# One batch-by-batch scan stage: first batch reordered, second batch's front beside it, last projection accumulated ahead, step sizes without VectorE's clamp

## The reference

```python
xn = _layernorm(x)
x = x + _L1_attn_ref(xn, ...) + _L1_ffn_ref(xn, ...)

# _L1_attn_ref (a Mamba block), in short
x, z = split(hidden @ in_proj_w.T)
u = silu(causal_conv(x, 4 taps) + conv_b)
dt_low, B, C = split(u @ x_proj_w.T)
delta = softplus(dt_low @ dt_proj_w.T + dt_proj_b)
h = exp(delta * A) * h + delta * B * u        # over 512 steps, 512 channels x 16 states
y = sum over states(h * C) + u * D
out = (y * silu(z)) @ out_proj_w.T

# _L1_ffn_ref: rows and weights are quantised in blocks of 32 to a 6-bit grid, then
out = xd @ wd.T + bias
```

## Time and profile before

| | |
|---|---|
| median of 3 runs | 2140.81 us (2137.47 to 2140.95) |
| profiled execution | 2136.74 us, its span 2134.9 us |
| busy, share of the span | PE 78%, DVE 71%, ACT 47%, POOL 44% |
| VectorE in 40 slices of 53.4 us, tenths | 6446464646465564545217988999999999999995 |
| granted TensorE clock in the same slices | 9999989898989899898686879788797969788576 |
| mix stage | from 1025.9 us on |
| first scan (L1462) | 1133.38 us |
| last gating (L1476) | 2112.34 us |

### The profile page before, as it was taken

The page is one execution under the profiler, slowest core; times in us unless marked ns, Lnnn a source line. Parts: engine busy times, 40 slices in busy tenths (PEclk is TensorE's granted clock), DMA queues, the critical chain, the costliest instruction groups (busy, mean ns, idle before and its releaser), DMA issues.

```text
span 2134.9 us, 22187 instructions
## 1 busy us (share of the span) xinstructions
PE 1675.0 (78%) x6696; PEld 747.9 (35%) x6696; DVE 1522.0 (71%) x2256; ACT 1009.9 (47%) x1542; POOL 943.0 (44%) x676
## 2 busy tenths in 40 slices
PE   7399999999999999999364768687686959687355
PEld 7252626253443535262121224132232414133022
DVE  6446464646465564545217988999999999999995
ACT  3026253443435252525234564757576575757441
POOL 2700000000000000000238778988898898988761
PEclk9999989898989899898686879788797969788576
DMA  5563636344261536260314132433324232432410
GB/s 182 203 103 103 103 100 98 114 76 137 55 134 58 89 105 102 97 113 10 107 59 149 51 111 89 142 123 120 120 99 157 93 125 89 139 128 98 150 50 10
DMA packets 103060, 223.84 MB, mean 105 GB/s; under 512 B 12641, under 2 KB 64994, under 8 KB 99282
## 3 DMA queue, kind: packets, MB, share of 16 engines
q1 hardware_dynamic: 99922, 214.69, 36.2%
q0 software_dynamic: 3072, 8.37, 1.1%
HBM read 169.56 MB, written 53.48 MB: 104 GB/s over the span
## 4 chain that ended last, share of the span: by engine, by line
DVE 22%; PE 14%; issue 7%; POOL 4%; POOLq 2%; DMA 1%; DVEq 1%; ACT 1%; SPq 0%; ACTq 0%
DVE ps L1462 16%; PE ps L1555 6%; DVE work L1468 5%; POOL work L1198 3%; PE ps L1580 2%; PE ps L1587 2%; PE ps L1589 1%; PE ps L1563 1%; PE ps L1591 1%; PE ps L1590 1%; PE ps L1572 0%; POOLq L1246 0%; DVEq L1435 0%; POOLq L1168 0%; DVE xn_step L1442 0%
## 5 line engine op out<-in xcount | busy, mean ns | idle before, releaser
L1198 POOL TENSOR_TENSOR work<-rep,bc 128x1024 f32<-128x1024 f32 x256 | 600.3, 2366 | 116.8 <-PE ps L1580 85.6
L1462 DVE TENSOR_TENSOR_SCAN ps<-ps,work 128x512 f32<-128x512 f32 x512 | 623.5, 1218 | 37.5 <-POOL work L1198 27.5
L1338 ACT ACTIVATE ps<-rep,a_neg 128x512 f32<-128x512 f32 x512 | 345.3, 687 | 315.0 <-DVE work L1468 313.8
L713 DVE TENSOR_REDUCE m<-ps 128x1 f32<-128x512 f32 x512 | 328.2, 686 | 160.3 <-PE ps L819 157.6
L636 ACT ACTIVATE prob<-ps 128x1024 f32<-128x1024 f32 x256 | 257.4, 1022 | 225.7 <-PE ps L843 223.8
L1468 DVE TENSOR_TENSOR work<-ps,bc 128x512 f32<-128x512 f32 x512 | 343.9, 672 | 0.0
L1580 PE MATMUL ps<-work,pick 128*32 128x512 f32 x1024 | 186.1, 810 | 185.3 <-DVE work L1468 185.3
L577 POOL TENSOR_TENSOR m_parts<-m,nil 128x16 bf16<-128x16 f32 x32 | 7.1, 222 | 604.8 <-DVE m L713 604.8
L1555 PE MATMUL ps<-xn_t,in_taps 128*128 128x510 f32 (+3 forms) x512 | 241.3, 627 | 2.2 <-ACT xn_t L1268 1.5
L819 PE MATMUL ps<-k_st,q_st 96*128 96x512 bf16 x512 | 201.0, 437 | 31.2 <-DVE m L713 24.1
L843 PE MATMUL ps<-q_st,k_st 99*128 99x512 bf16 x512 | 166.9, 424 | 0.7
(11 more groups left out here) (176 smaller groups left out, 2058.6 us busy)
## 6 DMA issues: line engine op xcount, KB each, us to landing
rep<-rep_rows SPq DMA_DIRECT2D x128, 512.0 KB, 5.8
w<-in_w SPq DMA_DIRECT2D x32, 1024.0 KB
bc<-bc_rows SPq DMA_DIRECT2D x32, 512.0 KB, 4.7
rep_rows<-inputs SPq DMA_DIRECT2D x32, 512.0 KB, 5.4
qk_parts<-parts SPq DMA_DIRECT2D x96, 128.0 KB
q_st<-qk_parts SPq DMA_DIRECT2D x96, 128.0 KB, 10.5
k_st<-qk_parts SPq DMA_DIRECT2D x96, 128.0 KB, 11.4
dispatch<-zeros SPq DMA_DIRECT2D x4, 1280.0 KB, 10.5
```

The lines of the kernel that those rows point to most:

```text
L713: nc.vector.tensor_reduce(m[:, g % 2, qt, 2 * pair + i:2 * pair + i + 1], ps[:, S0 + i, :], AX.X, ALU.max).then_inc(s_reduced, 1)
L1198: nc.gpsimd.tensor_tensor(work[:, n % WS, :, :], rep[:, g % RS, 2 * h:2 * h + 2, 1, :], bc[:, k, 0, :].unsqueeze(1).broadcast_to([P, 2, SE ...
L1338: nc.scalar.activation(state(m), rep[:, g % RS, 2 * h + i, 0, :], ACT.Exp, scale=a_neg[:, c, 2 * h + i, k:k + 1]).then_inc(decay_ready, 1)
L1462: nc.vector.tensor_tensor_scan(state(m), state(m), work[:, n % WS, i, :], 0.0, ALU.mult, ALU.add).then_inc(state_ready, 1)
```

## The change

- **First batch, other order.** VectorE takes the statistics before the tap weights, and quantises the weights after binade. ScalarE weighs batch 1's expert rows and makes the step sizes before u; the gate projections (z), their Silu and the copy of the turned weights stand behind softplus. TensorE turns the quantised rows before x_proj and projects z after the step sizes; the weights are turned into bank W_FIRST = 3. GpSimd gathers batch 1's rows right after root(0).
- **Second batch's front beside it.** Addition, root, statistics, normalise and transposes of batch 1 are ahead of the loop. LATE is gone: its chain runs at the same offsets as all others. A tiny Exp stands ahead of the loop on ScalarE.
- **Rep load in halves.** `decay` and `drive` wait for two of the four DMAs at each of a chunk's first two pieces.
- **Last output projection ahead.** `out_proj` is split into `out_bias` (one product for the two tiles of a bank, in all batches), `out_known` (quantised rows and x) and `out_gated`. In batch 7 bias, known parts and two gated chunks stand in pieces 20 to 23, the third chunk in pieces 28 to 31, and only the fourth behind the last gating. Every batch is stored in two halves.
- **No clamp on VectorE.** `binade` is one instruction. ScalarE computes max(p − 1, 0) of the power p (`over_one`, one piece before `scale_step`), and the two scalings add the 1 back in their bias. The weights' clamp stays.

```diff
-LATE = 5
...
+W_FIRST = 3
...
-FIRST_PE = {"w": 0, "turn_quant": (1, 2)}
-FIRST_ACT = {"w": 1, "quant": (2, 3), "weigh": 0}
-FIRST_DVE = {"statistics": 2}
-FIRST_POOL = {"add": 2, "root": 4}
+LAST_OUT, LAST_GATED = (20, 21, 22, 23), (28, 29, 30, 31)
...
+        rep_loaded = [[sem(f"rep_loaded_{c}_{h}") for h in range(2)] for c in range(RS)]
...
+            return [(f, n - (f - 1) * PIECES) for f in range(1, BATCH)]
...
+                                     rows.unsqueeze(1).broadcast_to([CH, QUADS, 2 * SEQ])).then_inc(rep_loaded[g % RS][j // 2], 16)
...
-                        sp.wait_ge(out_copied, b * HALVES)
-                        sp.dma_start(io["out"][b - 1].rearrange("(t p) c -> p t c", p=P), x2[:, (b - 1) % XS, :, :]).then_inc(out_stored, 16)
+                        rows = io["out"][b - 1].rearrange("(t p) c -> p t c", p=P)
+                        for h in range(HALVES):
+                            sp.wait_ge(out_copied, (b - 1) * HALVES + h + 1)
+                            sp.dma_start(rows[:, 2 * h:2 * h + 2, :], x2[:, (b - 1) % XS, 2 * h:2 * h + 2, :]).then_inc(out_stored, 16)
...
-                    if q % PER_CHUNK == 0:
-                        pool.wait_ge(rep_loaded[g % RS], (g // RS + 1) * BLOCKS * 16)
+                    if q % PER_CHUNK < 2:
+                        pool.wait_ge(rep_loaded[g % RS][h], (g // RS + 1) * BLOCKS // 2 * 16)
...
+                for i, value in enumerate((-1.0, -2.0 ** -22, 1.5 * 2.0 ** 20)):
+                    nc.gpsimd.memset(shifts[:, i:i + 1], value)
+                nc.gpsimd.memset(idle[:, :], 0.0)
...
                 root(0)
+                pool.drain()
+                place_gather(1)
+                gather(1, range(TT))
                 scale_down(0)
                 for k in range(GRID_STEPS):
                     to_grid(0, k)
                 scale_up(0)
-                pool.drain()
-                place_gather(1)
-                gather(1, range(TT))
+                add_experts(1)
+                root(1)
...
-                    if n == FIRST_POOL["add"]:
-                        add_experts(1)
-                    if n == FIRST_POOL["root"]:
-                        root(1)
...
-                        if f > 1:
...
+                        if at == POOL_AT["gather"]:
...
+                def over_one(f):
+                    act.wait_ge(step_ready, f + 1)
+                    if f == 0:
+                        act.wait_ge(set_up, 1)
+                    nc.scalar.activation(xn_step[:, :, :], xn_step[:, :, :], ACT.Relu, bias=shifts[:, 0:1])
...
+                    act.drain()
...
-                    nc.scalar.activation(nudge, xn_step[:, :, :], ACT.Copy, scale=-2.0 ** -22)
-                    nc.scalar.activation(xn_step[:, :, :], xn_step[:, :, :], ACT.Copy, scale=1.5 * 2.0 ** 20).then_inc(step_scaled, 1)
+                    nc.scalar.activation(nudge, xn_step[:, :, :], ACT.Identity, scale=-2.0 ** -22, bias=shifts[:, 1:2])
+                    nc.scalar.activation(xn_step[:, :, :], xn_step[:, :, :], ACT.Identity, scale=1.5 * 2.0 ** 20, bias=shifts[:, 2:3]).then_inc(step_scaled, 1)
...
                     copy_turned(0, k, k)
+                weigh_experts(1)
+                over_one(0)
+                scale_step(0)
                 for c in range(DC):
                     act.wait_ge(in_done, c + 1)
                     e = nc.scalar.activation(u[:, c, :], ps[:, 2 + c, :], ACT.Silu, bias=conv_b[:, c, :])
                 e.then_inc(u_ready, 1)
-                for c in range(DC):
-                    act.wait_ge(z_done, c + 1)
-                    nc.scalar.activation(sz[:, 0, c, :], ps[:, Z_FIRST[c], :], ACT.Silu).then_inc(z_taken, 1)
+                for k in range(KD):
+                    copy_quant(0, k, k)
                 copy_rows(0, 2)
-                scale_step(0)
                 for c in range(DC):
                     take_dt(0, c, DT_FIRST[c])
                 exponents(0)
                 softplus(0)
+                for c in range(DC):
+                    act.wait_ge(z_done, c + 1)
+                    nc.scalar.activation(sz[:, 0, c, :], ps[:, Z_FIRST[c], :], ACT.Silu).then_inc(z_taken, 1)
+                act.wait_ge(w_turned, 1)
+                nc.scalar.activation(fw_t[:, :, :], ps[:, W_FIRST, :].rearrange("p (k d) -> p k d", d=DM), ACT.Copy).then_inc(w_copied, 1)
+                normalise(1)
                 act.wait_ge(a_ready, 1)
+                nc.scalar.activation(idle[:, :], idle[:, :], ACT.Exp)
+                act.drain()
                 for n in range(BATCH * PIECES):
                     b, q = n // PIECES, n % PIECES
                     decay(b, q)
-                    if n == FIRST_ACT["w"]:
-                        act.wait_ge(w_turned, 1)
-                        nc.scalar.activation(fw_t[:, :, :], ps[:, TB[0], :].rearrange("p (k d) -> p k d", d=DM), ACT.Copy).then_inc(w_copied, 1)
...
-                        weigh_experts(1)
...
+                        if at == ACT_AT["step"] - 1:
+                            over_one(f)
...
                 def binade(f):
                     dve.wait_ge(scaled, f + 1)
-                    nc.vector.tensor_scalar(xn_step[:, :, :].bitcast(I32), xn[:, :, :].bitcast(I32), 0x7F800000, None, ALU.bitwise_and)
-                    dve.drain()
-                    cross = xn_step[:, :, :].rearrange("p t c -> p (t c)").rearrange("p (c i) -> p i c", i=2)
-                    nc.vector.tensor_scalar(cross, cross, 1.0, 4.0, ALU.max, ALU.min).then_inc(step_ready, 1)
+                    nc.vector.tensor_scalar(xn_step[:, :, :].bitcast(I32), xn[:, :, :].bitcast(I32), 0x7F800000, None,
+                                            ALU.bitwise_and).then_inc(step_ready, 1)
...
-                tap_weights()
-                dve.wait_ge(a_exp, 1)
-
-                nc.vector.tensor_scalar(a_neg[:, :, :, :], a_neg[:, :, :, :], -1.0, -1e-30, ALU.mult, ALU.min).then_inc(a_ready, 1)
                 statistics(0)
                 aggregate(0)
+                tap_weights()
                 block_max(0)
                 block_scale(0)
                 binade(0)
+                dve.wait_ge(a_exp, 1)
+
+                nc.vector.tensor_scalar(a_neg[:, :, :, :], a_neg[:, :, :, :], -1.0, -1e-30, ALU.mult, ALU.min).then_inc(a_ready, 1)
                 quantise_weights()
+                statistics(1)
+                aggregate(1)
...
-                    if n == FIRST_DVE["statistics"]:
-                        statistics(1)
-                    if n == FIRST_DVE["statistics"] + 1:
-                        aggregate(1)
...
+                def out_bias(bank):
+                    nc.tensor.matmul(ps[:, bank, :].rearrange("p (t d) -> p t d", d=DM), one_row, bias.unsqueeze(1).broadcast_to([1, 2, DM]),
+                                     start=True, stop=False)
...
+                def out_known(b, t, bank):
                     o = ps[:, bank, (t % 2) * DM:(t % 2) * DM + DM]
...
                     for k in range(KD):
                         nc.tensor.matmul(o, quant_t[:, b % 2, k, t * P:(t + 1) * P], fw_t[:, k, :], start=False, stop=False)
...
+                    nc.tensor.matmul(o, sb["ident"][:, :], x2[:, b % XS, t, :], start=False, stop=False)
...
+                def out_gated(b, t, bank, cs):
+                    o = ps[:, bank, (t % 2) * DM:(t % 2) * DM + DM]
+                    for c in cs:
+                        x = nc.tensor.matmul(o, sz[:, b % 2, c, t * P:(t + 1) * P], out_w[:, c, :], start=False, stop=(c == DC - 1 and t % 2 == 1))
+                    if cs[-1] == DC - 1 and t % 2:
                         x.then_inc(out_done, 1)
+
+                def out_proj(b, t, bank):
+                    if t % 2 == 0:
+                        out_bias(bank)
+                    out_known(b, t, bank)
+                    out_gated(b, t, bank, range(DC))
...
                     pe.wait_ge(w_quant, 1)
+                    pe.wait_ge(dt_taken, DC - 1)
...
+                            x = nc.tensor.transpose(ps[:, W_FIRST, k * DM + t * P:k * DM + (t + 1) * P], fw_raw[:, t, k * P:(k + 1) * P],
...
                 for c in range(DC):
                     in_proj_taps(2 + c, c, range(TAPS), in_done)
-                for c in range(DC):
-                    in_proj(Z_FIRST[c], c, z_done)
+                pe.wait_ge(quant_ready, 1)
+                for k in range(KD):
+                    turn(k, k, quant_turned)
                 project_bc(0, 2)
                 pe.wait_ge(rows_copied, 1)
                 for c in range(DC):
                     project_dt(0, c, DT_FIRST[c])
+                pe.wait_ge(quant_copied, KD)
+                for c in range(DC):
+                    in_proj(Z_FIRST[c], c, z_done)
+                turn_weights()
                 pe.wait_ge(diag_ready, 1)
                 pe.wait_ge(z_taken, DC)
                 pe.wait_ge(dt_taken, DC)
                 pe.wait_ge(set_up, 1)
+                pe.wait_ge(xn_ready, 2)
+                for k in range(KD):
```

(17 more changed lines are left out.)

58 lines of the change are left out of this document (18 added, 40 removed).

## The result

The changed kernel takes 2073.48 us (median of four runs, 2069.07 to 2077.0), against 2139.92 for the kernel before, run beside it. The ratio is 0.969, 95% interval 0.9668 to 0.9712. The forecast was 2080, in a range of 2066 to 2092, so the gain of 66.4 us is 6.6 more than the sum of 59.8.

A forecast was written before the change was run, and what follows sets the result against it. TensorE was taken to bound pieces 0 to 16 of steady batches, with waits at front, seam and tail. Front 17.6, batch 0 9.8, batch 1 15.9, bias 2, tail 14.5 sum to 59.8 us: 2080, range 2066 to 2092.

The forecast's parts named there:

- (a): Front: batch 0's statistics ahead of the tap weights; 1.5 us gained (0 to 4.4), after 2.9 lost to engines blocking.
- (b): Front: gate projections (z) go behind on TensorE, eight passes for quantised rows replace them; 5.6 us gained (5.0 to 6.0).
- (c): Front: scale_step(0) no longer between x_rows and the step-size projections on ScalarE; 0.6 us gained (0 to 0.7).
- (d): Front: GpSimd's first input no longer queued behind quantisation and batch 1's gathers after the Ln; 7.0 us gained (6.5 to 7.1).
- (e): Front: GpSimd's first product starts on half of the rep load; 2.9 us gained (2.0 to 3.0).
- (f): Front: Exp table loaded ahead of the wait; 0 gained, as the first scan waited for the product, not a decay.
- the front is held: Rival: TensorE waits for the quantised rows ahead of x_proj, 6 us lost, 2086 us; chance 0.07.
- Batch 0: Batch 1's statistics 1.8, decay wait 2.5, small scaling 1.7, GpSimd waits 1.2, clamp 2.6: 9.8 us gained (6 to 12).
- the seam stays: Rival: GpSimd's scale_down or inputs for batch 1 come late again, about 11 us, 2091; chance 0.17, wholly or half.
- The clamp in batches 1 to 6: Removing VectorE's clamp there gains 0 of 12.1 us, since it stands inside TensorE's unbroken stretch.
- chief rival: The clamp counts in batches 1 to 6 too, because VectorE bounds them: 12 us less, 2068; chance 0.17.
- The clock: Rival: TensorE's clock left lower for 8.6 us' worth of work in seven batches eats all 60 us; slower 0.03.

The follow-up runs named there:

- taps_first: The changed kernel with the tap weights ahead of the statistics again: mix stage 1046.2 us against 1042.7, first scan 3.1 us later.
- taps_late: The changed kernel with the tap weights held until the root is done: median 2070.18 us, ratio 0.9691; mix stage 1042.5 us against 1042.7.
- rep_full: The changed kernel with decay and drive waiting for all four rep DMAs at a chunk's first piece: mix stage 1045.9 us against 1042.7.
- clamp_back: The changed kernel with VectorE's clamp put back and ScalarE's Relu dropped: median 2076.71 us; mix stage 1047.6 us against 1042.7.
- tail_back: The changed kernel with batch 7's whole output projection behind the last gating, bias still one product: mix stage 1060.6 us against 1042.7, tail 21.7 against 7.4.
- late_back: The changed kernel with batch 1's chain five pieces late again: mix stage 1054.4 us against 1042.7, batch 1's distance 130.23 against 118.73.
- bias_old: The changed kernel with the old output projection in batches 0 to 6 (gated rows first, one bias product a tile): mix stage 1049.8 us against 1042.7.
- relieved pair: The changed kernel with bias, quantised rows and x left out of batches 0 to 6's output projections, without and with VectorE's clamp: mix stage 1033.6 and 1046.6 us.
- queue: The changed kernel with x_proj ahead of the output projection's third and fourth tile: 2063.39 us, ratio 0.9657; mix stage 1033.7 us, with VectorE's clamp 1046.5.

## Why the prediction was right, and where a size was off

- **The front.** (a) 1.5 forecast, 2.2 measured (24.3 to 22.1 us up to the first normalise); the mechanism is shown by taps_first and taps_late. Three of the four operations were expected to pay, 2.9 in all; two did, by 0.9 each, and the power by 0.13, and taps_late puts the loss at 2.1. (b) 5.6 and 5.6, (c) 0.6 and 0.6, (d) 7.0 and 7.0, (e) 2.9 and 2.8, all by the timeline's landmarks, (e) confirmed by rep_full. (f) gains nothing, though only because the load comes later than the decay needs it. The rival that the front is held is out: x_proj waits for u alone.
- **Batch 0.** 9.8 and 9.9, but that they agree so closely is luck. Four terms held: the clamp (2.6 forecast, 2.8 by clamp_back), the statistics, and the waits of 2.48 and 1.04 us, which are gone. One didn't: the small scaling was to give back 1.7 us and takes 2.10 where it took 1.86, again beside a product of GpSimd's. In its place the binade, which was to stay as it was, gave back 1.5: it took 2.54 and takes 1.03. The binade in the timeline of the kernel before:

```profile
1172.63 2.54 DVE L1442 TENSOR_SCALAR xn_step<-xn 128x1024 int32<-128x1024 int32 x1
```

Both in that of the changed kernel:

```profile
1127.02 2.10 DVE L1446 TENSOR_SCALAR absmax<-absmax 128x32 f32<-128x32 f32 x1
...
1139.71 1.03 DVE L1452 TENSOR_SCALAR xn_step<-xn 128x1024 int32<-128x1024 int32 x1
```

- **Batch 1.** 15.9 and 17.5, but 16.4 against tail_back's execution of the same code, whose distance is 119.81: up to 1.1 us of it is where the clock rose. LATE alone is 11.5 (late_back). The new projection has a share, 2.4 by bias_old; the remaining 3.6 were not taken apart. The rival that the seam stays is out.
- **The clamp in batches 1 to 6** at 0, the choice on which the forecast rested against its chief rival: held. By clamp_back the distances differ by -0.1 to 0.4, less than those of two executions of the same code do, and bias_old shows 0 in the steady ones. The rival, 12 us more, would have come near with another queue of TensorE's (10.7 us behind batch 0 in the relieved pair, 10.1 in that of queue).
- **The bias: the term that was mis-sized.** I had "0.35 a batch, six times: 2 us (0 to 6)". bias_old puts it at 7.1 for the stage, 1.2 a steady batch, over my upper bound; against distances like tail_back's it would be about 5. By my own prices a bank saves 0.4 (1.3 less 0.9); a batch has two banks, so this should have been 0.8 a batch, and 0.35 is that of one. Measured, a bank saves 0.59: only 0.19 in the bias itself (twice 0.62 less 1.05), the rest in the products beside it. This term and batch 1 make 5.1 of the 6.5 us between forecast and measurement, and up to 2.1 of these 5.1 are the clock's, as tail_back shows.
- **VectorE's waits** were to grow from 1.0 to 3.6 and are 2.4 (0.49, 0.88, 1.02). The same error: the shorter projection took 1.2 of them away; in bias_old they are 3.6 (0.49, 2.06, 1.02).
- **The tail.** 14.5 and 15.2, by tail_back 14.3. The products took 3.4 us where 3.3 were forecast, copy and store 3.2 (from 2072.04 to the end) where 4.0 were. The cover held: GpSimd waits up to 6.96 us in batch 7 and VectorE none for it. The longest of these waits of GpSimd, in the changed kernel's timeline, beside the earlier trace rows:

```profile
1996.42 4.66 POOL L1199 TENSOR_TENSOR work<-rep,bc 128x1024 f32<-128x1024 f32 x2 [6.96 <-PE ps L1586]
```

- **The clock** did not fall: 0.98 in the full stretch, 0.854 over the span, 0.853 before. The rival looked only at its level; what moves the steady batches is where in the batch it rises, which the prediction doesn't have.

## What to carry to other kernels

Ask of each instruction taken off the engine with the highest busy share what that engine waits for next in the same stretch: here the same instruction was worth 4.9 us of the stage with one order of TensorE's queue and 12.8 with another. Measure between two landmarks that repeat (here the statistics of each batch), not whole times: the stages ahead scattered by 9 us, more than most of the terms. Where TensorE bounds such a batch, compare also where in it the granted clock rises: here that moved single batches by up to 1.1 us and undid most of a gain of 2.6 us in the front. A term that is worked out for one bank or tile has to be counted out over the batch before it is summed.
